# Scattering the experts' results with an addition, so that the combination of a fused attention and mixture-of-experts block reads two arrays

## The reference

```python
x = x + _L0_conv_ref(_ln_c(x), qkv_w, rpb, proj_w, proj_b)      # the attention's result, "x1" below
t = _to_tokens(x)                                               # (8, 3136, 128)
t = t + _L0_ffn_ref(_ln_t(t), W_router, W1, b1, W2, b2)
x = _from_tokens(t, x)

def _L0_ffn_ref(x, W_router, W1, b1, W2, b2):
    topk_p, topk_i = jax.lax.top_k(softmax(x_flat @ W_router), 2)
    topk_p = topk_p / topk_p.sum(axis=-1, keepdims=True)
    out = 0
    for e in range(E):
        out = out + combine[:, e:e + 1] * (relu(x_flat @ W1[e] + b1[e]) @ W2[e] + b2[e])
```

## Time and profile before

| | |
|---|---|
| median of 3 runs | 3058.23 us |
| profiled execution | 3044.93 us, of which the span from first to last instruction 3043.1 us |
| TensorE busy | 2705.5 us, 89% of the span |
| VectorE / ScalarE / GpSimd busy | 75% / 70% / 52% |
| attention and routing | from 0 to about 2240 us |
| tables and first loads of the experts' stage | about 2240 to 2286 us |
| experts | 2286 to about 2881 us |
| combination | about 2882 to 3043 us |
| DMA | 378.50 MB, 124 GB/s over the span |

### The profile page before, as it was taken

The page is one execution under the profiler, slowest core; times in us unless marked ns, Lnnn a source line. Parts: engine busy times, 40 slices in busy tenths (PEclk is TensorE's granted clock), DMA queues, the critical chain, the costliest instruction groups (busy, mean ns, idle before and its releaser), DMA issues. The chain is left out here.

```text
span 3043.1 us, 112867 instructions
## 1 busy us (share of the span) xinstructions
PE 2705.5 (89%) x31450; PEld 2390.9 (79%) x31451; DVE 2277.6 (75%) x12559; ACT 2115.7 (70%) x5724; POOL 1586.8 (52%) x2024
## 2 busy tenths in 40 slices
PE   4799999999999999999999999999909999999733
PEld 2799998899989998999899989999806766667522
DVE  2688887788878887788778878878837878877655
ACT  1588787787878787887788868888727777777400
POOL 2145555455545554555455545555635777777600
PEclk9999999999999999999999999999959999999855
DMA  2555656565556655665555555666455444444399
GB/s 50 144 119 120 127 123 125 110 125 124 124 114 124 124 125 114 122 125 123 117 122 124 123 117 123 123 122 130 102 101 97 97 95 95 96 96 94 102 323 313
DMA packets 706127, 378.50 MB, mean 124 GB/s; under 512 B 414608, under 2 KB 662064, under 8 KB 705584
## 3 DMA queue, kind: packets, MB, share of 16 engines
q1 hardware_dynamic: 652784, 235.97, 40.1%
q10 hardware_dynamic: 24192, 81.67, 9.3%
q0 software_dynamic: 28608, 54.48, 6.0%
HBM read 233.43 MB, written 98.11 MB: 109 GB/s over the span
## 5 line engine op out<-in xcount | busy, mean ns | idle before, releaser
L980 ACT ACTIVATE pr<-sc,nmx 128x100 f32<-128x100 f32 x3136 | 924.1, 369 | 61.6 <-DVE nmx L655 60.7
L890 POOL TENSOR_TENSOR oml<-om 128x256 f16<-128x256 f32 x784 | 480.4, 613 | 893.2 <-DVE om L685 877.6
L510 PE MATMUL bank<-vwin,pt 100*128 100x65 f32 x6272 | 803.8, 271 | 29.0 <-DVE om L685 28.4
L655 DVE CUSTOM_DVE_ANT_0 sc<-bank,near 128x100 f32<-128x100 f32 x3136 | 634.1, 257 | 239.0 <-PE bank L488 199.3
L510 PEld LDWEIGHTS bank<-vwin,pt 100*128 100x128 f32 x6272 | 771.0, 194 | 46.8 <-ACT pt L988 39.8
L488 PE MATMUL bank<-kimg,qexp 128*128 (+2 forms) x9408 | 627.0, 215 | 40.2 <-issue 22.2
L488 PEld LDWEIGHTS bank<-kimg,qexp 128*128 128x128 bf16 (+1 forms) x9408 | 559.9, 100 | 87.5 <-issue 55.6
L988 ACT ACTIVATE pt<-bank 100x512 f32<-100x512 f32 x784 | 461.2, 588 | 211.4 <-PE bank L497 193.5
L1347 POOL DMA_INDIRECT yrows<-ye,meta x420 | 452.9, 1078 | 173.9 <-issue 106.7
L858 POOL DMA_INDIRECT xrows<-rows,idx x448 | 425.5, 950 | 114.4 <-issue 74.3
L497 PE MATMUL bank<-cst_sb,pr 128*100 128x128 f32 x3136 | 476.1, 275 | 0.0
(11 more groups left out here) (136 smaller groups left out, 3916.6 us busy)
## 6 DMA issues: line engine op xcount, KB each, us to landing
vwin<-v_pix SPq DMA_DIRECT2D x1120, 60.5 KB
near<-bias_rows ACTq DMA_DIRECT2D x112, 600.0 KB, 4.9
y<-yrows SPq DMA_DIRECT2D x112, 224.0 KB, 4.2
qexp<-qring SPq DMA_DIRECT2D x896, 14.0 KB
v_pix<-vrow SPq DMA_DIRECT2D x56, 225.8 KB
xin<-in_x SPq DMA_DIRECT2D x56, 224.0 KB
xres<-in_x SPq DMA_DIRECT2D x112, 112.0 KB
x<-xres SPq DMA_DIRECT2D x112, 112.0 KB
```

Source lines behind the costliest of these rows:

```text
L510: mm = pe.matmul(ps_av[m % 2][:, 2 * t + blk, :], pt[:, m % 2, 2 * t + blk, :], vwin[:, st, 2 * u + t, 64 * blk:64 * blk + 65], start=True ...
L655: i = v.tensor_tensor_reduce(out=sc[:, ring(m, par), k, :], in0=ps_s[m % 2][:, k, :], in1=near[:, st, ct, k, :], scale=-1.0, scalar=-MASKE ...
L890: g.tensor_tensor(oml[:, st, u], om[:, st, u], om_h[:, st, u], ALU.subtract).then_inc(s["oml_done"], 1)
L980: i = a.activation(pr[:, r, k, :], sc[:, r, k, :], ACT.Exp, bias=nmx[:, r, k:k + 1], scale=-1.0)
```

## The change

The scatters of the experts' results get an addition, done by the DMA (`compute_op=ALU.add`), so each row's old content in DRAM is read, added to and written back. The rows must hold something first: the first-choice array gets the attention's result, written from `xtr` by ScalarE's queue (`put_x1`, step 5 of each pair), the second-choice array gets zeros from a new SBUF tile `blank` (`put_zero`, step 6), and the padding's 7,680 rows get zeros in one DMA at the start. `turn_out` now also waits until `put_x1` of the pair before has landed, since `xtr` has one buffer. In the combination the load of `xo` is gone, and VectorE's addition from PSUM and `xo` becomes a copy from PSUM (`evict`). The number of scatters stays 420.

```diff
--- before.py
+++ after.py
@@ -173,6 +173,7 @@
         one = asb("one", [HALF, 1])
         xt = asb("xt", [C, 2, TOK])
         xtr = asb("xtr", [HALF, QT, C])
+        blank = asb("blank", [128, C])
         wr_sb = asb("wr_sb", [C, E])
         wrm = asb("wrm", [C, E])
         strict_b = asb("strict_b", [128, HALF], BF16)
...
@@ -400,6 +401,8 @@
                     sp.wait_ge(s[f"x1_store{st}"], 16 * PAIRS)
                 load_tokens(PAIRS - 1, (PAIRS - 1) % 2)
                 sp.wait_ge(s["v_store"], V_DMAS * PAIRS)
+                sp.wait_ge(s["y_x1"], 16 * PAIRS)
+                sp.wait_ge(s["y_zero"], 16 * PAIRS + 16)
                 for st in range(2):
                     sp.wait_ge(s[f"x1_store{st}"], 16 * PAIRS)
 
@@ -599,6 +602,7 @@
                 v.memset(qexp[:, 1].rearrange("p s t h q -> p (s t h q)"), 0.0).then_inc(s["zeroed"], 1)
                 v.memset(vrow[:, :, 64:65], 1.0).then_inc(s["pad_zero"], 1)
                 v.memset(ones_b[:], 1.0)
+                v.memset(blank[:], 0.0).then_inc(s["y_blank"], 1)
                 v.memset(eps[:], 1e-5)
                 v.memset(one[:], 1.0)
                 v.wait_ge(s["cst_in"], 16)
@@ -921,6 +925,19 @@
                 a.wait_ge(s["w_in"], 48)
                 a.activation(qkv_w_sb[:, 0:C], qkv_w_sb[:, 0:C], ACT.Copy, scale=float(HD) ** -0.5).then_inc(s["w_scaled"], 1)
 
+                a.wait_ge(s["y_blank"], 1)
+                a.dma_start(yrows[2 * NTOK:2 * NTOK + (E + DUMMY) * T, :].rearrange("(p g) c -> p g c", p=128),
+                            blank[:].unsqueeze(1).to_broadcast([128, (E + DUMMY) * 4, C])).then_inc(s["y_zero"], 16)
+
+                def put_x1(Q, par):
+                    a.wait_ge(s["r_turned"], Q + 1)
+                    dst = bass.AP(yrows.tensor, Q * (TOK * C), [[C, HALF], [HALF * C, QT], [1, C]])
+                    a.dma_start(dst, xtr[:]).then_inc(s["y_x1"], 16)
+
+                def put_zero(Q, par):
+                    dst = bass.AP(yrows.tensor, NTOK * C + Q * (TOK * C), [[C, HALF], [HALF * C, QT], [1, C]])
+                    a.dma_start(dst, blank[0:HALF].unsqueeze(1).to_broadcast([HALF, QT, C])).then_inc(s["y_zero"], 16)
+
                 def a_square(I):
                     a.wait_ge(s["xc_done"], I + 1)
                     a.activation(sq[:], xc[:], ACT.Square).then_inc(s["sq_done"], 1)
@@ -999,6 +1016,8 @@
                 def turn_out(Q, par):
                     a.wait_ge(s["r_t"], Q + 1)
                     if not early(Q, 1):
+                        a.wait_ge(s["y_x1"], 16 * Q)
+                    if not early(Q, 1):
                         a.wait_ge(s["r_xn"], Q)
                         a.wait_ge(s["r_stat"], Q)
                     a.activation(xtr[:].rearrange("p n c -> p (n c)"), ps_a[0:HALF, :], ACT.Copy).then_inc(s["r_turned"], 1)
@@ -1034,7 +1053,7 @@
                     a.wait_ge(s["r_lo"], Q + 1)
                     a.activation(rowsb[:, par, 1, :, 0:2 * C], rowsb[:, par, 0, :, 0:2 * C], ACT.Copy).then_inc(s["r_both"], 1)
 
-                R_STEPS = {4: turn_out, 7: signs, 9: normal_rows, 10: high_rows, 12: exp_gap}
+                R_STEPS = {4: turn_out, 5: put_x1, 6: put_zero, 7: signs, 9: normal_rows, 10: high_rows, 12: exp_gap}
 
                 def body(I, J, par):
                     for m in range(UPP):
...
@@ -1170,8 +1188,6 @@
                         .then_inc(s[f"m_meta{r}"], 16)
                 moe_tiles(sp, moe)
 
-                for r in range(ZR):
-                    sp.dma_start(xo[:, r, :], x1[:, r * TOK:(r + 1) * TOK]).then_inc(s[f"z_x{r}"], 16)
                 for r in range(XR):
                     sp.wait_ge(s[f"m_sc{r}"], 16 * 4 * ((NT - r + XR - 1) // XR))
 
@@ -1181,8 +1197,6 @@
                     for j, dst in ((0, y0), (1, y1)):
                         src = bass.AP(yrows.tensor, c * (TOK * C) + j * (NTOK * C), [[QT * C, HALF], [1, QT * C]])
                         sp.dma_start(dst[:, r].rearrange("p n c -> p (n c)"), src).then_inc(s[f"z_x{r}"], 16)
-                    if not early(c, ZR):
-                        sp.dma_start(xo[:, r, :], x1[:, bass.ds(c * TOK, TOK)]).then_inc(s[f"z_x{r}"], 16)
                 out_tiles(sp, fetch)
                 for par in range(2):
                     sp.wait_ge(s[f"z_store{par}"], 16 * (CT // 2))
@@ -1314,26 +1328,25 @@
                 gated(NT - 1, 0, last)
 
                 def add_rows(c, r):
-                    v.wait_ge(s[f"z_x{r}"], 48 * (c // ZR) + 48)
+                    v.wait_ge(s[f"z_x{r}"], 32 * (c // ZR) + 32)
                     if not early(c, 2):
                         v.wait_ge(s["z_t"], c - 1)
                     v.tensor_tensor(ys[:, r % 2], y0[:, r], y1[:, r], ALU.add).then_inc(s["z_sum"], 1)
 
-                def add_x1(c, r):
+                def evict(c, r):
                     par = r % 2
                     v.wait_ge(s["z_t"], c + 1)
                     if not early(c, 2):
                         v.wait_ge(s[f"z_store{par}"], 16 * (c // 2))
-                    v.tensor_tensor(oo[:, par].rearrange("c (p n) -> c n p", n=QT),
-                                    bank[6 + par][:, 0:TOK].rearrange("c (n p) -> c n p", n=QT),
-                                    xo[:, r].rearrange("c (p n) -> c n p", n=QT), ALU.add).then_inc(s["z_out"], 1)
+                    v.tensor_copy(oo[:, par].rearrange("c (p n) -> c n p", n=QT),
+                                  bank[6 + par][:, 0:TOK].rearrange("c (n p) -> c n p", n=QT)).then_inc(s["z_out"], 1)
 
                 def combine(c, r):
                     add_rows(c, r)
                     if not early(c, 1):
-                        add_x1(c - 1, (r - 1) % ZR)
+                        evict(c - 1, (r - 1) % ZR)
                 out_tiles(v, combine)
-                add_x1(CT - 1, ZR - 1)
+                evict(CT - 1, ZR - 1)
 
             @block.gpsimd
             def _(g):
@@ -1345,7 +1358,7 @@
                     g.nop(nofuse=True)
                     for q in range(4):
                         g.indirect_dma_start(out=yrows, out_offset=bass.IndirectOffsetOnAxis(ap=meta[:, r, q, 1:2].bitcast(U32), axis=0),
-                                             in_=ye[:, r % XR, q, :], in_offset=None).then_inc(s[f"m_sc{r % XR}"], 16)
+                                             in_=ye[:, r % XR, q, :], in_offset=None, compute_op=ALU.add).then_inc(s[f"m_sc{r % XR}"], 16)
                 moe_tiles(g, spread)
 
             @block.scalar
```

More of the change, by code:

```diff
@@ L221, in build @@
             c_small r_small r_wrm r_const r_first r_x0 r_x1 r_t r_turned r_logit r_stat r_ve r_pow r_nmr r_lg r_top r_atf r_hot r_hots
-            r_gap r_gapr r_eg r_share r_gate r_pos r_prod r_idxf r_idx r_cap r_xn r_hi r_lo r_dest r_both r_sc0 r_sc1""".split()
+            r_gap r_gapr r_eg r_share r_gate r_pos r_prod r_idxf r_idx r_cap r_xn r_hi r_lo r_dest r_both r_sc0 r_sc1 y_blank y_x1 y_zero""".split()
         s = {n: sem(n) for n in names}
@@ L1111, in build @@
         ys = sb("ys", [HALF, 2, QT, C])
-        xo = sb("xo", [C, ZR, TOK])
         oo = sb("oo", [C, 2, TOK])
```

## The result

Median 3248.53 us (3244.77 to 3251.0) against 3058.53 on the same chip: the ratio is 1.0623, 95% interval 1.0602 to 1.0645. The change makes the kernel 190 us slower; 29 us faster was forecast.

What follows compares the result with a forecast made beforehand. It took TensorE to bound attention and experts, GpSimd close behind, and the DMA engines to bound the combination. Terms -35 + 0 + 1 + 2 + 3 = -29 us from the 3058.23 median gave 3029 us, range 3012 to 3130.

Steps and rivals of the forecast that it cites:

- The scatters: Experts' stage: the addition costs 0.11 us per scatter, hidden by TensorE's chain, so 0 in the sum.
- The cover: Experts' stage: a long scatter once a tile read as a wait for TensorE's chain, slack of 0.1 us per scatter.
- Rival 1: Experts' stage: GpSimd becomes the pace, 0.22 us more per scatter, +45 us, about 3074; chance 0.32.
- point of decision, 0.18 us: Experts' stage: from 0.18 us more per scatter, the scatters' cost decides (420 x 0.07 = 29 us).
- rivals 1 and 2: Scatters: 0.22 us more each, about 3074, chance 0.32; or 968 ns doubled, +360 us, about 3390, chance 0.13.
- The combination: Last stage: without the xo loads, at 318 GB/s, it shortens by 35 us (28 to 39).
- Chunks near 2.1 us: Combination: sign of being right, chunks near 2.1 us with the DMA share still near 1.
- Rival 3: Combination: loads were hidden anyway, the store's landing holds it and stays at 4.3 us; about 3060, chance 0.07.
- +1 for the last scatter's landing: After the last scatter: its landing includes a read and stands bare, +1 us, bounded by 2.0 us.
- The start: ScalarE's issue of the 7,680-row fill holds it to about 36 us, delaying GpSimd's root; +3 us (0 to 7).
- Attention: Two more DMA issues a pair on ScalarE, mostly hidden, +2 us (0 to 38); DMA share 0.59 to 0.63.
- rival 4: Attention: ScalarE's added issues are bare, each pair loses 0.7 us, +36 us, about 3065; chance 0.06.

Runs made afterwards that it cites:

- e5: Changed kernel with a plain scatter (no addition) and four output buffers `oo`, each with its own semaphore, in place of two; 3024.08 us, ratio to before 0.9906.
- e9: e5 with eight buffers each for y0 and y1 in place of four; 3004.50 us, ratio to before 0.9851.
- e6: Kernel before the change with four output buffers `oo`, each with its own semaphore; 3054.92 us, ratio to before 0.9996.
- e1: Changed kernel with plain scatters in place of adding ones, all else as changed; 3035.68 us, ratio to before 0.9915.
- e7: Kernel before with `blank`, its fills, `put_x1` and `put_zero` added, plain scatter, three arrays read in the combination; 3062.55 us, ratio to before 1.0015.
- e10: Kernel before with 42 of 56 x1 chunks loaded during the experts' stage, four `oo`, eight buffers each for y0 and y1; 3022.87 us, ratio to before 0.9892.
- e11: Kernel before with eight buffers each for y0, y1 and xo and four for `oo`; 3054.29 us, ratio to before 0.9998.

## Why the prediction was wrong

**The scatters: the step that failed.** The text took "0.11 us, hidden by TensorE's chain: **0**" for the addition. It is 0.59 us in the median and 0.51 in the mean, and 420 x 0.51 = 214 us of the run are its price. The 0.11 came from the slope between two kinds of plain scatter, 1.7 ns a row; within one kind the slope is 1.1, and the part of the price that goes with the rows is 0.17 us, of the same order as the 0.11. The slope could not show a cost that an instruction has once, and that is 0.42 of the 0.59. Both ends were written down, nothing and 968 ns, with "Nothing shown speaks for either"; between ends so far apart a price near zero needed a reason why a new kind of instruction should cost what the old kind does per row and nothing besides.

The cover was misread too, though not in size. "The tile's first scatter" at 2524.54 is a third one, and its length is no wait for TensorE's chain that a trace shows; GpSimd had no idle time but the 0.30 us gaps in the whole stage. The 0.1 us of slack per scatter came out as 0.08. That the number is so near is luck.

**Rival 1 is what happened, at a price outside its bounds** (0.11 to 0.35 us, up to 3130). Its formula holds: 420 x (1.589 + 0.30) = 793 us against 793.6 measured. Its point of decision, 0.18 us, was passed three times over. The price lies between rivals 1 and 2, a gap that neither held, so the range missed.

The rule that an add in the DMA, since it needs two source reads, about halves the rate of a ReduceScatter (the Trainium skill, Collectives: The Full Stack, on why ReduceScatter is half of AllGather) had the direction right. A scatter here takes 1.61 times as long. Its slope per row, from 1.1 to 2.4 ns, is somewhat more than doubled; whether that is a second read no run shows, and the part without rows is not in that rule.

**The combination: right in kind, too large.** Forecast -35 (28 to 39; 56 half cycles are 158 us and not 157, which moves the 39 by less than 1), measured -18.7. The term was priced at the rate of three arrays and supposed that the DMA engines stay the limit. They did not: the two `oo` buffers became it (9.9 us, e5), then the four buffers of y (20.5 us, e9). "Chunks near 2.1 us" were 2.35, and a DMA share near 1 was no sign that the engines had no room. Rival 3 was wrong about the landing, which fell from 4.3 to 3.4 us, and about the stage before the change (e6), but the chain that it named, through the store alone, is what holds the stage after it. With the depth that it needs, the stage loses 48.8 us (163.3 to 114.5), more than was forecast, since x1's packets were dearer than those of y and the latter get cheaper without them. Of the +1 for the last scatter's landing nothing shows: the stage is 144.6 us with the addition and 144.9 without (e1).

**The start.** GpSimd's first root is 2.9 us later than in the earlier trace rows, as the +3 had it, but not by the way described, so the size was luck. From the timeline after:

```profile
16.14 0.67 ACTq L929 DMA_DIRECT2D yrows<-blank  x1
...
26.19 8.69 POOL L844 DMA_DIRECT2D gath<-pad_rows  x16 [2.33 <-DMA pad_rows<-pad]
34.99 1.06 POOL L879 TENSOR_TENSOR rstd<-ve,powc 112x4 f32<-112x4 f32 x1
```

ScalarE's issue of the fill took 0.67 us and not some 20, and its first square starts at 19.44 as before. GpSimd's own loads wait for one another: `gath` starts at 26.19 in place of 23.02, after 2.33 us of idle time until `pad_rows` has landed. The root stands at 34.99 to 35.25 in after, e1, e7 and e9, which have the fill, and at 32.02 to 32.07 in before, e10 and e11, which don't.

**Attention.** TensorE's share did not move, the DMA share is 0.63 as worked out, and rival 4 falls. GpSimd's first scatter by expert moves from 198.6 to 201.7 us and its last from 2238.5 to 2243.9: 3 us from the start and 2 from the attention, as forecast, in two profiles. e7, with both terms in it, gives 4.6 us with an interval from 1.5 less than nothing to 10.7 (of 3053): the forecast 5 lies in it, and so does 0. The 2 to 5 us at a like clock fit it too.

**Were the addition free**, the changed kernel would be e1: 3035.68 us, 24 under before, against 3029 forecast. That is inside the range, with the combination's gain some 16 us short.

## What to carry to other kernels

An instruction with a new mode is a new instruction: its price per instruction is bounded by nothing in the old one's rows, so where an engine has 0.1 us of slack per instruction, measure one before anything is built on it. When bytes are taken out of a stage that the DMA engines fill, count the buffers again: rings that covered the old rate may be the next limit, the gain stays hidden until they are deeper, and a DMA share of 0.96 does not show it. A transfer whose data are ready early can be moved to a stage with idle DMA engines, which gave here what the addition in DRAM was to give, without its price.

## What the runs showed of the hardware

An adding scatter goes out as one packet of 512 B for each of its 128 rows, where a plain one had 16 packets of 4 KB: the scatters' queue has 75,648 packets in place of 28,608, 112 more for each of 420. The time that the addition takes of GpSimd did not depend on the bytes of a row (256 or 512 B, 1558 ns both).

Loads did not cost the same per byte: before the change, of the time of all 16 engines, packets of x1 took 3.50 us per MB and packets of y 3.18; without x1, those of y took from 3.63 us (four buffers, two for the output) to 2.90 (eight and four). The rate at full DMA share was 320 GB/s with x1 (e11) and 365 without (e9).

In 14 profiles of these kernels TensorE, busy all of the time from 106 to 126 us, had the higher level of its clock in eight and the lower in six, and the first scatter of the experts' results started 9 to 12 us later in the latter.
